# Routing of two mixture-of-experts layers: slot lists inverted by batched 16-bit one-hots instead of one 32-bit pair per tile

## What is computed

```python
# first expert layer: every token goes to its 2 best of 8 experts, no limit
logits = xn @ Wr + br
top_vals, top_idx = top_k(logits, 2)
w = softmax(top_vals)
y = sum over e of (gelu(xn @ W1[e] + b1[e]) @ W2[e] + b2[e]) * w_full[..., e]

# second expert layer: the best of 8 experts, C = 977 places each
probs = softmax(x @ gate_w + gate_b)
idx = argmax(probs)
pos = (cumsum(one_hot, axis=0) * one_hot).sum(-1) - 1
kept = pos < C
```

## Time and profile before

| what | value |
|---|---|
| runs | 5372.98 us median of 3 (5372.53 to 5374.61) |
| span of the profiled execution | 5371.9 us |
| median of the runs less that span | 1.1 us |
| TensorE busy | 4172.9 us (78%) |
| VectorE busy | 3413.4 us (64%) |
| ScalarE busy | 1663.0 us (31%) |
| GpSimd busy | 2167.4 us (40%) |
| mean granted TensorE clock | 0.850 |

### The profile page before, as it was taken

How to read it: one execution, slowest core, us unless ns; L and a number is a source line. 1 busy time by engine, 2 the same in 40 slices (tenths; PEclk the granted TensorE clock), 3 DMA queues, 4 the chain that set the end, 5 groups by cost and what they waited for, 6 DMA issues and landing times. The chain is left out here.

```text
span 5371.9 us, 86748 instructions
## 1 busy us (share of the span) xinstructions
PE 4172.9 (78%) x27330; PEld 3017.8 (56%) x27331; DVE 3413.4 (64%) x7289; ACT 1663.0 (31%) x2903; POOL 2167.4 (40%) x2194
## 2 busy tenths in 40 slices
PE   3477777777777777746999945999999999769992
PEld 2355555555555555534888833666656666458872
DVE  6466666666666666687555577888888888640115
ACT  1233333333333333321222264333333333121121
POOL 1477777777777777700666600000000000202220
PEclk9678777777777887756999966999999999759996
DMA  4766666666666666651566543444444444323333
GB/s 122 189 168 170 167 165 170 170 162 170 170 165 167 170 169 163 158 207 68 193 200 199 183 139 84 81 85 89 81 81 88 87 81 85 88 86 121 100 118 103
DMA packets 946866, 733.83 MB, mean 137 GB/s; under 512 B 703102, under 2 KB 832054, under 8 KB 944599
## 3 DMA queue, kind: packets, MB, share of 16 engines
q1 hardware_dynamic: 835851, 433.62, 31.3%
q0 software_dynamic: 104144, 289.95, 20.0%
q10 hardware_dynamic: 6652, 7.32, 0.4%
HBM read 483.39 MB, written 92.34 MB: 107 GB/s over the span
## 5 line engine op out<-in xcount | busy, mean ns | idle before, releaser
L1288 POOL DMA_INDIRECT gat_rows<-h_rows,gat_sources x1664 | 1577.0, 948 | 509.2 <-issue 485.5
L1526 PE MATMUL gat_sum_ps<-gat_rows,gat_onehot 128*128 128x265 f32 x3328 | 1167.6, 510 | 3.2 <-DVE gat_rows L1418 2.4
L1526 PEld LDWEIGHTS gat_sum_ps<-gat_rows,gat_onehot 128*128 128x128 f32 x3328 | 792.9, 250 | 190.4 <-issue 5.7
L2055 ACT CAST gnn_z<-build_ps 128x392 bf16<-128x392 f32 x992 | 473.4, 486 | 847.7 <-PE build_ps L2070 842.3
L1997 DVE TENSOR_TENSOR onehot_low<-dense_codes,dense_iota_bf 128x2048 bf16<-128x2048 bf16 x496 | 604.0, 1218 | 2.6 <-PE build_ps L2070 2.6
L2080 PE MATMUL back_ps<-zb_pieces,gnn_z 128*128 128x384 bf16 x3038 | 567.1, 327 | 0.0
L2102 PE MATMUL front_ps<-x_res_wide,front_rows 128*128 128x448 bf16 x2604 | 562.5, 353 | 0.0
L1976 POOL DMA_INDIRECT front_rows<-zf_piece_rows,vrow_nodes x62 | 64.8, 1046 | 1231.2 <-PE front_ps L2102 1221.0
L1418 DVE TENSOR_TENSOR gat_rows<-gat_rows,gat_numerators_ps 128x1024 f32<-128x1024 f32 x416 | 502.0, 1207 | 0.0
L2471 PE MATMUL moe_hidden_ps<-moe_rows_T,moe_w 128*128 128x256 f32 (+1 forms) x1408 | 459.9, 483 | 2.7 <-DVE moe_rows_T L2512 0.8
L2070 PEld LDWEIGHTS build_ps<-onehot_high,onehot_low 128*128 128x128 bf16 x7936 | 339.4, 98 | 204.6 <-issue 38.5
(11 more groups left out here) (366 smaller groups left out, 5160.4 us busy)
## 6 DMA issues: line engine op xcount, KB each, us to landing
moe_w<-in_L_ffn_W SPq DMA_DIRECT2D x112, 512.0 KB
gat_targets<-gat_step_targets SPq DMA_DIRECT2D x104, 512.0 KB
moe_w<-in_L_ffn_w SPq DMA_DIRECT2D x32, 1024.0 KB
gat_rows<-h_rows,gat_sources POOLq DMA_INDIRECT x1664
moe_rows_out<-moe_slot_zeros SPq DMA_DIRECT2D x36, 512.0 KB
gat_flags<-gat_tile_flags SPq DMA_DIRECT2D x104, 128.0 KB
normal_rows<-moe_xn_all SPq DMA_DIRECT2D x14, 896.0 KB
mid_taken<-moe_rows_out SPq DMA_DIRECT2D x14, 896.0 KB, 7.3
```

The costliest lines, as they stand in the source:

```text
L1288: pool.indirect_dma_start(out=g[:, b, t, :], out_offset=None, in_=T.h[:, :], in_offset=bass.IndirectOffsetOnAxis(ap=idx[:, b, t:t + 1], ax ...
L1526: last = pe.matmul(po[:, s % BANKS, 0:W], o[:, b, s * SUB + t, :], g[:, b, s * SUB + t, :], start=t == 0, stop=t == SUB - 1)
L2055: nc.scalar.copy(AT[:, k % 2, :, CHUNK * c:CHUNK * (c + 1)], pb[:, c % 2, 0:CHUNK * NT].rearrange("p (u h) -> p h u", u=CHUNK)).then_inc(a ...
```

## The change

The edits are in `route`, with two constants in `setup`.

1. Both matmuls of the counts take 16-bit operands: the product with `valid` is written as the 16-bit `mask`, and `upper_b` and `ones_b` are 16-bit copies of the constants.
2. The one-hots are 16-bit and made in batches: 7 batches of 14 token tiles in moe1, 5 batches of 10 in moe2 (50 places for 49 tiles, the last one empty). The tiles of a batch lie in pairs, so that the innermost two elements are two tiles' values. A batch takes one compare for `ot`, one for `ol` and one multiplication on VectorE.
3. A token is carried as two numbers that 16 bits hold exactly, its lane plus one and its tile plus one. `ov` has both halves: ScalarE scales `ot` by the lane (L2395), VectorE multiplies it by the tile number (L2369). TensorE multiplies 128 x (2 x `tiles`) columns per token tile, and waits for both halves.
4. The ring is two batches, with one semaphore step per batch and engine.
5. `pi` has two parts; the token's number is put together from them by three operations where one stood.
6. The array `own` of token numbers is gone (one operation per choice); five small operations prepare the 16-bit arrays.

```diff
@@ -248,6 +248,8 @@
             c.mark(dve.memset(C.ones[:, :], 1.0))
             c.mark(dve.memset(C.eps[:, :], EPS))
             c.mark(dve.memset(C.one[:, :], 1.0))
+            c.mark(dve.tensor_scalar(C.upper_b[:, :], tri_i[:, :], 0.0, None, ALU.is_gt))
+            c.mark(dve.memset(C.ones_b[:, :], 1.0))
             dve.wait_ge(ld, 16 * len(loads))
 
             for a in range(2):
@@ -2198,14 +2200,20 @@
     io = k.sem(f"{tag}_route_iota")
     oh = k.sem(f"{tag}_slot_onehots_ready")
     ou = k.sem(f"{tag}_slot_onehots_used")
+    om = k.sem(f"{tag}_slot_tiles_compared")
+    oa = k.sem(f"{tag}_slot_lanes_scaled")
     tiles = groups * tok // P
-    RING = 4
+    M = choices * NT
+    PAIRS = 7 if choices == 2 else 5
+    BATCHES = -(-M // (2 * PAIRS))
+    MP = BATCHES * PAIRS * 2
     with ExitStack() as ctx:
         lg = k.sb(ctx, f"{tag}_logits", [P, NT, X])
         t0 = k.sb(ctx, f"{tag}_t0", [P, NT, X])
         pv = k.sb(ctx, f"{tag}_pv", [P, NT, X])
         mk = k.sb(ctx, f"{tag}_masks", [P, choices, NT, X])
         both = k.sb(ctx, f"{tag}_both", [P, NT, X])
+        mask = k.sb(ctx, f"{tag}_mask_bf", [P, NT, X], BF16)
         mx = k.sb(ctx, f"{tag}_mx", [P, choices, NT])
         ix = k.sb(ctx, f"{tag}_ix", [P, NT])
         dd = k.sb(ctx, f"{tag}_dd", [P, NT])
@@ -2223,15 +2231,19 @@
         gc = k.sb(ctx, f"{tag}_gcmp", [P, groups, X])
         gw = k.sb(ctx, f"{tag}_gw", [P, groups])
         sl_i = k.sb(ctx, f"{tag}_slot_int", [P, NT], I32)
-        hi = k.sb(ctx, f"{tag}_slot_tile", [P, choices, NT])
-        lo = k.sb(ctx, f"{tag}_slot_lane", [P, choices, NT])
-        own = k.sb(ctx, f"{tag}_token_number", [P, choices, NT])
-        ol = k.sb(ctx, f"{tag}_onehot_lane", [P, RING, P])
-        ot = k.sb(ctx, f"{tag}_onehot_tile", [P, RING, tiles])
+        hi = k.sb(ctx, f"{tag}_slot_tile", [P, NT])
+        hi_b = k.sb(ctx, f"{tag}_slot_tile_bf", [P, MP], BF16)
+        lo_b = k.sb(ctx, f"{tag}_slot_lane_bf", [P, MP], BF16)
+        io_b = k.sb(ctx, f"{tag}_iota_bf", [P, P, 2], BF16)
+        m1_b = k.sb(ctx, f"{tag}_token_tile_bf", [P, MP], BF16)
+        p1 = k.sb(ctx, f"{tag}_token_lane", [P, 1])
+        ol = k.sb(ctx, f"{tag}_onehot_lane", [P, 2, PAIRS, P, 2], BF16)
+        ot = k.sb(ctx, f"{tag}_onehot_tile", [P, 2, PAIRS, tiles, 2], BF16)
+        ov = k.sb(ctx, f"{tag}_onehot_values", [P, 2, PAIRS, 2, tiles, 2], BF16)
         inv = k.sb(ctx, f"{tag}_slot_token", [P, tiles])
         free = k.sb(ctx, f"{tag}_slot_free", [P, tiles])
         spare = k.sb(ctx, f"{tag}_spare_row", [P, tiles])
-        pi = k.ps(ctx, f"{tag}_slot_ps", [P, tiles])
+        pi = k.ps(ctx, f"{tag}_slot_ps", [P, 2, tiles])
         pk = k.ps(ctx, f"{tag}_rank_ps", [P, 512])
         pt = k.ps(ctx, f"{tag}_total_ps", [P, 512])
         block = ctx.enter_context(nc.Block())
@@ -2248,7 +2260,12 @@
             c = Chain(dve, ch)
             tt, ts = dve.tensor_tensor, dve.tensor_scalar
             c.link(tt(lg[:, :, :], logits[:, :, :], over(bias[:, :]), ALU.add))
-            c.link(dve.memset(zero[:, :], 0.0))
+            c.mark(dve.memset(zero[:, :], 0.0))
+            c.mark(dve.memset(hi_b[:, :], -1.0))
+            c.mark(dve.memset(lo_b[:, :], 0.0))
+            c.mark(dve.tensor_copy(io_b[:, :, :], C.iota[:, :].unsqueeze(2).to_broadcast([P, P, 2])))
+            c.mark(ts(m1_b[:, :], C.iota[:, 0:MP], 1.0, None, ALU.add))
+            c.mark(ts(p1[:, :], C.wiota[:, 0:1], 1.0, None, ALU.add))
             c.link(ts(valid[:, :], C.wiota[:, :], float(S.N) - 0.5, None, ALU.is_lt))
 
             def first_of(values, m, out):
@@ -2289,7 +2306,7 @@
                 c.link(dve.tensor_copy(weight[:, 0, :], mx[:, 0, :]))
                 c.link(dve.tensor_copy(both[:, :, :], mk[:, 0, :, :]))
 
-            c.link(tt(both[:, :, :], both[:, :, :], wide(valid[:, :]), ALU.mult))
+            c.link(tt(mask[:, :, :], both[:, :, :], wide(valid[:, :]), ALU.mult))
             dve.nop(nofuse=True).then_inc(mr, 1)
             dve.wait_ge(rk, 1)
             c.link(dve.tensor_copy(tot[:, :, :], pt[:, 0:NT * X].rearrange("p (n x) -> p x n", x=X)))
@@ -2328,24 +2345,33 @@
                 c.link(tt(sl[:, :], sl[:, :], dd[:, :], ALU.add))
                 c.link(dve.tensor_copy(sl_i[:, :], sl[:, :]))
                 c.link(ts(sl_i[:, :], sl_i[:, :], P.bit_length() - 1, None, ALU.arith_shift_right))
-                c.link(dve.tensor_copy(hi[:, n, :], sl_i[:, :]))
-                c.link(dve.scalar_tensor_tensor(out=lo[:, n, :], in0=hi[:, n, :], scalar=-float(P), in1=sl[:, :],
+                own = slice(n * NT, (n + 1) * NT)
+                c.link(dve.tensor_copy(hi[:, :], sl_i[:, :]))
+                c.mark(dve.scalar_tensor_tensor(out=lo_b[:, own], in0=hi[:, :], scalar=-float(P), in1=sl[:, :],
                                                 op0=ALU.mult, op1=ALU.add))
-                c.link(dve.scalar_tensor_tensor(out=hi[:, n, :], in0=hi[:, n, :], scalar=1.0, in1=kp[:, :],
+                c.link(dve.scalar_tensor_tensor(out=hi[:, :], in0=hi[:, :], scalar=1.0, in1=kp[:, :],
                                                 op0=ALU.add, op1=ALU.mult))
-                c.link(ts(hi[:, n, :], hi[:, n, :], -1.0, None, ALU.add))
-                c.link(ts(own[:, n, :], C.wiota[:, :], float(n * S.ROWS + 1), None, ALU.add))
-
-            for m in range(choices * NT):
-                n, i = m // NT, m % NT
-                if m >= RING:
-                    dve.wait_ge(ou, m - RING + 1)
-                ts(ol[:, m % RING, :], C.iota[:, :], lo[:, n, i:i + 1], None, ALU.is_equal)
-                ts(ot[:, m % RING, :], C.iota[:, 0:tiles], hi[:, n, i:i + 1], own[:, n, i:i + 1],
-                   ALU.is_equal, ALU.mult).then_inc(oh, 1)
-            dve.wait_ge(ou, choices * NT)
-            c.link(ts(free[:, :], pi[:, :], 0.5, None, ALU.is_lt))
-            c.link(ts(inv[:, :], pi[:, :], -1.0, None, ALU.add))
+                c.link(ts(hi_b[:, own], hi[:, :], -1.0, None, ALU.add))
+
+            for b in range(BATCHES):
+                at = slice(b * PAIRS * 2, (b + 1) * PAIRS * 2)
+
+                def pairs(v, w):
+                    return v[:, at].rearrange("p (u t) -> p u t", t=2).unsqueeze(2).to_broadcast([P, PAIRS, w, 2])
+
+                def numbers(w):
+                    return io_b[:, 0:w, :].unsqueeze(1).to_broadcast([P, PAIRS, w, 2])
+                if b >= 2:
+                    dve.wait_ge(ou, b - 1)
+                tt(ot[:, b % 2, :, :, :], pairs(hi_b, tiles), numbers(tiles), ALU.is_equal).then_inc(om, 1)
+                tt(ol[:, b % 2, :, :, :], pairs(lo_b, P), numbers(P), ALU.is_equal)
+                dve.wait_ge(om, b + 1)
+                tt(ov[:, b % 2, :, 1, :, :], ot[:, b % 2, :, :, :], pairs(m1_b, tiles), ALU.mult).then_inc(oh, 1)
+            dve.wait_ge(ou, BATCHES)
+            c.mark(ts(free[:, :], pi[:, 1, :], 0.5, None, ALU.is_lt))
+            c.link(ts(inv[:, :], pi[:, 1, :], float(P), -float(P + 1), ALU.mult, ALU.add))
+            c.link(tt(inv[:, :], pi[:, 0, :], inv[:, :], ALU.add))
+            c.link(ts(inv[:, :], inv[:, :], -1.0, None, ALU.max))
             c.link(ts(spare[:, :], C.iota[:, 0:tiles], float(P), C.wiota[:, 0:1], ALU.mult, ALU.add))
             c.link(ts(spare[:, :], spare[:, :], float(choices * S.ROWS + 1), None, ALU.add))
             c.link(tt(spare[:, :], spare[:, :], free[:, :], ALU.mult))
@@ -2362,17 +2388,29 @@
                 nc.scalar.activation(kp[:, :], dd[:, :], ACT.Exp).then_inc(eo, 1)
             else:
                 nc.scalar.activation(pos[:, :, :], pv[:, :, :], ACT.Exp).then_inc(eo, 1)
+            for b in range(BATCHES):
+                act.wait_ge(om, b + 1)
+                if b >= 2:
+                    act.wait_ge(ou, b - 1)
+                nc.scalar.activation(ov[:, b % 2, :, 0, :, :].rearrange("p u w t -> p u (w t)"),
+                                     ot[:, b % 2, :, :, :].rearrange("p u w t -> p u (w t)"),
+                                     ACT.Copy, scale=p1[:, 0:1]).then_inc(oa, 1)
 
         @block.tensor
         def _(pe):
             pe.wait_ge(mr, 1)
-            flat = both[:, :, :].rearrange("p n x -> p (n x)")
-            pe.matmul(pk[:, 0:NT * X], C.upper[:, :], flat, start=True, stop=True)
-            pe.matmul(pt[:, 0:NT * X], C.ones[:, :], flat, start=True, stop=True).then_inc(rk, 1)
-            for m in range(choices * NT):
-                pe.wait_ge(oh, m + 1)
-                pe.matmul(pi[:, :], ol[:, m % RING, :], ot[:, m % RING, :], start=m == 0,
-                          stop=m == choices * NT - 1).then_inc(ou, 1)
+            flat = mask[:, :, :].rearrange("p n x -> p (n x)")
+            pe.matmul(pk[:, 0:NT * X], C.upper_b[:, :], flat, start=True, stop=True)
+            pe.matmul(pt[:, 0:NT * X], C.ones_b[:, :], flat, start=True, stop=True).then_inc(rk, 1)
+            for b in range(BATCHES):
+                pe.wait_ge(oh, b + 1)
+                pe.wait_ge(oa, b + 1)
```

(8 more changed lines are left out.)

## The result

The changed kernel takes **5332.41 us** (median of 4 runs, 5329.96 to 5334.36), the kernel before took 5372.75 us beside it (4 runs, 5371.35 to 5374.61). The ratio is 0.9925, with a 95% interval of 0.9911 to 0.9940: about 40 us or 0.75% less, near the 5334 us that were forecast. The profiled execution has a span of 5330.3 us.

What follows compares the result with a forecast made beforehand. VectorE was taken to bound both routing loops. Loops -22.9 and -12.5, counts -4.2, small operations +0.8 sum to -38.8 us: span 5371.9 to 5333.1, with 1.1 for the median 5334 us, range 5329 to 5343.

Steps and rivals of the forecast that it cites:

- The compares: VectorE's three operations per batch in the routing loops: 0.522 ns per element, 2.79 us a batch in moe1, 1.55 in moe2.
- rival B: Paired layout misses two elements per cycle in the loops: all three operations 5359 us, multiplication alone 5341; chance 0.07.
- +4 us bound for lost overlaps: Upper bound in the loops if waits stop neighbouring VectorE operations overlapping: 36 operations at 0.11 us more each.
- ScalarE's half: Scaling by the lane in each batch: about 1.60 us in moe1, 0.82 in moe2, hidden beside VectorE's work.
- TensorE: Loop matmuls hidden under VectorE except the last batch: 1.5 us at clock 1.00 in moe1, 1.3 at 0.50 in moe2.
- Rival A: TensorE's clock stays at 0.50 in the first loop: last batch 1.3 us longer, buffer waits 0.6, 5336 us; chance 0.20.
- The loops: Both routing loops: first 21.2 us against 44.13, -22.9; second 9.25 against 21.77, -12.5.
- The counts: Counting matmuls ahead of each loop in 16 bits: 1.05 us instead of 3.13, -2.1 per routing, -4.2 us.
- Small operations: Preparing operations ahead of the loops, removed ones and two more behind each loop: together +0.8 us.
- Behind the routings: Gather and first matmul move earlier with the row lists; the expert layer finds the same cold clock: costed at nothing.
- C: Clock rises later in moe1's first expert groups, about 5 us a group; 10 groups would give 5384 us; chance 0.02.
- D: Loop gain partly returns as later DMA and compute meet in other phases, a few us either way; chance 0.05.

Runs made afterwards that it cites:

- e2: The changed kernel with batches of 2 token tiles instead of 14 and 10: 5364.76 us, ratio 0.9979 to the kernel before.
- e3: 16-bit one-hots without batches, three VectorE operations per token tile, nothing on ScalarE, counts on 16 bits: 5404.67 us, ratio 1.0053 to the kernel before.
- e5: The changed kernel with ScalarE's scaling by the lane given back to VectorE: 5350.22 us, ratio 0.9950 to the kernel before.
- e7: The changed kernel with the lane's compare written a second time per batch, into an unread buffer: 5349.15 us, ratio 0.9949 to the kernel before.
- e0: The changed kernel once more, no edit: 5336.7 us, ratio 0.9929 to the kernel before.
- e1: The kernel before with only the counting matmuls on 16-bit operands, loops untouched: 5370.23 us, ratio 0.9990 to the kernel before.
- e8: The same kernel as e5, measured once more: 5352.73 us, ratio 0.9960 to the kernel before.
- e6: The changed kernel with VectorE's multiplication by the tile number moved to GpSimd: 5353.53 us, ratio 0.9956 to the kernel before.

## Why the prediction was right

*The compares.* 2.79 us a batch were forecast from the earlier trace rows, 2.78 measured, and 0.97 and 1.08 us for the durations. In moe2 1.55 was forecast, and 1.55 measured (4746.65 - 4745.10). The multiplication, which no row showed, runs at the compares' rate: 0.97 us, so rival B didn't come. The +4 us bound for lost overlaps was not needed. The rate even held at 224 elements, in e2.

*The cost that went was one per instruction.* e3 shows it: in 16 bits 98 tiles at three instructions each cost 18 us more than before at two, and by its pair in two sizes the kernel before paid 0.32 us of 0.44 for the instructions, as the prediction had it. The weighing of the Trainium skill (VectorE: DVE Perf Modes, The TRN2 errata) came out as the rows had said. Its formula fits the batch, 2.75 us against 2.78, and not the short operations with a number per lane, so that by it alone the first loop would have gained 5 us instead of 22.8.

*ScalarE's half.* 1.60 us forecast, 1.60 measured, in moe2 0.82 and 0.83. It ended 0.26 us ahead of the multiplication. What it saved is shown by e5: on VectorE it costs 8.7 us. In batches of two it isn't free: in e2 TensorE waited for it.

*TensorE.* The last batch showed 1.66 us of waiting (1.5 forecast), 1.34 in moe2 (1.3). The clocks came as taken, 1.00 in the first loop and 0.50 in the second. Rival A was true of the first 6 us: two batches of matmuls ran at 0.50, VectorE waited 0.2 us for a buffer, once, and the clock rose behind it. A's price of 1.3 us for the last batch was never due. That A can happen is shown by e2 and e3, in which the clock stayed at 0.50 through the whole first loop.

*The loops.* -22.9 and -12.5 us forecast, -22.8 and -12.6 measured. e7 confirms the premise of it all, that a microsecond of VectorE there is one of the kernel's: compares reckoned at 10.8 us made the loops 10.5 longer, and the median 12 longer than e0's, from another comparison.

*The counts.* -2.1 us each forecast; 3.13 - 0.99 = 2.14 measured, and e1 has it alone.

*Small operations.* +0.8 forecast; the stretches ahead are 0.3 and 0.1 us shorter than e1's, which has the counts alone, and those behind 0.4 longer each, so about +0.4.

*Behind the routings.* The gather and the first matmul moved ahead with the list. The matmul waited 13.06 us for its rows, 12.12 in the earlier trace rows, and the first group's clock was again 0.58:

```profile
2507.37 0.95 POOL L2471 DMA_INDIRECT moe_rows<-normal_rows,moe_slot_source  x1 [145.22 <-POOLq L2210]
...
2516.23 1.12 PE L2499 MATMUL moe_turn_ps<-ident,moe_rows 128*128 128x128 f32 x4 [13.06 <-DMA moe_rows<-normal_rows,moe_slot_source]
```

The layer took 763.6 us for 763.5: neither C nor D. (The sign given for C, more than one group at the low clock, would have misled: a stretch of 8 us from 32 us behind the first gather runs at 0.79, in the kernel before as well.) Costing the layer at nothing was right for this kernel, but less safe than the 0.07 for C and D together says. Two of the kernels tried, e3 and e5 (again in e8), lost 7 us there, by a way other than C's: gaps in TensorE's own issue with the clock at 1.00. That is a fifth of the gain, from edits no closer to the layer than this change.

Sum: -38.8 forecast, -39.3 measured in the routings. The -2.2 of the dense layer were in nobody's sum. That the median lies within 2 us of the forecast is finer than the measurement: the same kernel took 4 us more in the next comparison.

## What to carry to other kernels

A loop of small VectorE operations costs mostly by the instruction, here 0.21 us for some 120 elements, whether the output has 32 bits or 16. Find out what batching does to the other side: here it paid only together with 16 bits, which halved TensorE's passes and kept the compare's rate, and 16 bits paid only with batches. Make the batch long enough that the ring of hand-offs is shorter than one batch. An idle ScalarE is a free place for a part of it; an idle GpSimd is not, if its operation shuts VectorE's out.

## What the runs showed that was not expected

- GpSimd's two-input multiplication of 1568 16-bit elements shuts VectorE's 16-bit compare out until it is done (0.97 us become 3.58). Its own record is 3.58 us too, for an operation that took VectorE 0.97; how much of that is waiting isn't shown.
- TensorE's granted clock can stay at 0.50 for a whole loop in which its rows look busy: 25.81 of 37 us in e2, 35.98 of 62 in e3 and 21.17 of 22 in the old second loop. In the old first loop it rose within 6 us.
- An operation with one 16-bit source and a number per lane, 1568 elements written with a gap between blocks, took 1.02 us, no less than a compare with two sources (0.97).
- The first expert layer takes either 762 to 765 or 771 us, reproducibly by kernel (766.6 in e6), with identical code in it. In the longer form TensorE has a gap of 0.29 us in its issue at every second group. What brings it on wasn't found.
